# One attention and sign-weight feed-forward block: second-half projections one step later, six down-weight signs moved past attention, and pairwise probability sums on GpSimd

## The reference

```python
x = layernorm(x + attn(x))      # x is (2, 1024, 512) float32, 16 heads of 32
x = layernorm(x + ffn(x))

# attn: qkv = x @ w_qkv.T + b_qkv
#       scores = q @ k.T / sqrt(32), causal mask, softmax over the keys, @ v
#       out @ w_out.T + b_out
# ffn:  relu(x @ sign(up_weight).T * up_scale) @ sign(down_weight).T
#       * down_scale * output_scale          (512 -> 2048 -> 512)
```

## Time and profile before

| | us |
|---|---|
| three runs | 834.71, 837.71, 842.72 (median 837.71) |
| the profiled execution | 842.53, of which the span from first to last instruction is 840.8 |
| PE busy | 770.7 (92%) |
| DVE busy | 453.1 (54%) |
| ACT busy | 324.1 (39%) |
| POOL busy | 268.4 (32%) |

### The profile page before, as it was taken

How to read it: one execution, slowest core, us unless ns; L and a number is a source line. 1 busy time by engine, 2 the same in 40 slices (tenths; PEclk the granted TensorE clock), 3 DMA queues, 4 the chain that set the end, 5 groups by cost and what they waited for, 6 DMA issues and landing times.

```text
span 840.8 us, 11785 instructions
## 1 busy us (share of the span) xinstructions
PE 770.7 (92%) x4176; PEld 524.9 (62%) x4176; DVE 453.1 (54%) x1086; ACT 324.1 (39%) x631; POOL 268.4 (32%) x415
## 2 busy tenths in 40 slices
PE   6899889999999998999989958899999999999994
PEld 5688646555655465555634425478787877878883
DVE  3276455675656657657556644363339327633614
ACT  5200435454544554545545644732222223221211
POOL 5801513314223134132240241153235234423333
PEclk9999889999999999999977979999999999999997
DMA  8937452542734335425375453021001200100101
GB/s 299 295 83 216 134 139 89 141 128 61 200 101 100 116 112 143 112 79 161 89 189 164 143 196 113 1 66 63 24 13 38 88 25 13 38 2 0 51 1 50
DMA packets 44619, 85.72 MB, mean 102 GB/s; under 512 B 4880, under 2 KB 13584, under 8 KB 44432
## 3 DMA queue, kind: packets, MB, share of 16 engines
q1 hardware_dynamic: 35536, 79.72, 31.8%
q10 hardware_dynamic: 9024, 5.24, 2.2%
HBM read 55.33 MB, written 29.36 MB: 101 GB/s over the span
## 4 chain that ended last, share of the span: by engine, by line
PE 72%; DVE 14%; DMA 5%; issue 4%; ACT 2%; POOL 1%; SPq 1%; ACTq 0%; DVEq 0%; POOLq 0%
PE ps_heads L952 9%; PE ps_sum L946 8%; PE ps_unit L891 8%; PE ps_proj L853 7%; PE ps_proj L992 6%; PE ps_score L928 6%; DVE heads_sb L750 6%; PE ps_score L1007 6%; PE ps_unit L966 6%; PE ps_unit L992 5%; PE ps_heads L1007 3%; PE ps_sum L1007 3%; DVE heads_sb L752 2%; DMA qk_parts<-parts 2%; DVE ps_unit L724 2%
## 5 line engine op out<-in xcount | busy, mean ns | idle before, releaser
L636 ACT ACTIVATE probs<-ps_score 128x512 f32<-128x512 f32 (+3 forms) x360 | 171.2, 491 | 193.4 <-PE ps_score L928 185.6
L891 PE MATMUL ps_unit<-stack 96*128 96x512 f32 (+3 forms) x384 | 138.3, 369 | 14.1 <-DVE maxes L728 7.9
L724 DVE CUSTOM_DVE_ANT_0 ps_unit<-ps_unit,causal 128x128 f32<-128x128 f32 (+3 forms) x256 | 122.7, 502 | 50.4 <-PE ps_unit L891 49.2
L928 PE MATMUL ps_score<-stack 98*128 98x512 f32 (+2 forms) x360 | 136.6, 388 | 8.9 <-ACT probs L636 5.7
L559 POOL TENSOR_SCALAR_AFFINE_SELECT probs<-probs 128x128 f32<-128x128 f32 x256 | 74.7, 298 | 212.6 <-ACT probs L636 209.2
L583 POOL TENSOR_TENSOR hid_low<-hid_raw,hid_high 128x512 fp32r<-128x512 f32 x64 | 85.0, 1328 | 175.7 <-DVE hid_high L803 169.5
L728 DVE TENSOR_REDUCE maxes<-ps_unit 128x1 f32<-128x512 f32 x128 | 88.2, 689 | 85.3 <-PE ps_unit L891 84.3
L891 PEld LDWEIGHTS ps_unit<-stack 96*128 96x128 f32 x384 | 75.6, 198 | 48.7 <-DVE maxes L728 16.1
L928 PEld LDWEIGHTS ps_score<-stack 98*128 98x128 f32 x360 | 71.4, 199 | 39.6 <-ACT probs L636 20.5
L803 DVE CAST hid_high<-hid_raw 128x512 fp32r<-128x512 f32 x64 | 27.1, 425 | 121.1 <-ACT hid_raw L681 120.8
L553 POOL TENSOR_TENSOR parts<-qk_full,parts 128x512 fp32r<-128x512 f32 x32 | 41.3, 1292 | 155.8 <-ACT parts L618 155.8
(11 more groups left out here) (162 smaller groups left out, 1174.3 us busy)
## 6 DMA issues: line engine op xcount, KB each, us to landing
stack<-qk_parts SPq DMA_DIRECT2D x96, 256.0 KB, 5.0
qk_parts<-parts SPq DMA_DIRECT2D x32, 512.0 KB, 2.8
v_all<-h_even ACTq DMA_DIRECT2D x16, 256.0 KB, 3.2
v_rows<-v_all SPq DMA_DIRECT2D x8, 512.0 KB, 4.6
heads_t<-heads_sb SPq DMA_DIRECT2D x16, 256.0 KB, 2.7
raw<-up_w SPq DMA_DIRECT2D x8, 512.0 KB, 4.3
raw<-down_w SPq DMA_DIRECT2D x8, 512.0 KB, 3.8
heads_raw<-heads_t SPq DMA_DIRECT2D x4, 1024.0 KB, 5.7
```

What stands on the lines that cost most here:

```text
L636: nc.scalar.activation(probs[:, (NP * s + n) % RING, 0:width], score_bank(s, n)[:, off:off + width], ACT.Exp, scale=SCALE).then_inc(s_exp, 1)
L724: nc.vector.tensor_tensor_reduce(ps_unit[n % 3][:, 0:width], ps_unit[n % 3][:, 0:width], causal[:, HALF - width:], 1.0, NEG, ALU.add, ALU.max,
L891: nc.tensor.matmul(ps_unit[n % 3][:, 0:width], stack[s % 2][0:96, 1, f, h, i % 4 * P:(i % 4 + 1) * P], stack[s % 2][0:96, 0, c, h, 0:width ...
L928: nc.tensor.matmul(score_bank(s, n)[:, 0:width + off], stack[s % 2][0:98, 0, j // 4, h, j % 4 * P:(j % 4 + 1) * P], stack[s % 2][0:98, 1, ...
```

## The change

It has four parts. **Projections:** `BLOCK` now names for each block how many steps ahead it is made. Blocks 2 and 3 (the second half) are made one step ahead, at the start of the step, blocks 0 and 1 two steps ahead, later in the step. Before the first score only two blocks of step 1 are left, and step 6 makes two blocks of step 7. The loads of the second batch of x stand later in SP's order, and the weights of a new group are taken up in another place. **Units:** all units of the second query half with the first key half (c = 0) come before those with the second key half (c = 1), so that the first 32 units need three blocks and the last 16 the fourth; the table `MAXIMA` starts at slot 10.2 rather than 0.5, and the two shifts stand at 35.9 and 51.9 rather than 27.9 and 48.2. **Row sums:** for the four full key tiles of the second query half, POOL adds the probabilities of two key tiles (`pairs`, four tiles of 128x512 at a time), and one row-sum matmul per head takes the sum of the two. **Late part:** six of the down signs stand behind the start of the feed-forward part (with the weights stored in another order, `down_at`), `up` and `down` of chunk 0 wait for each sign apart; the first fetch of heads stands in step 6 and goes to a buffer of its own, the output projection has two banks in step 7, and its slots are 7 to 31.

```diff
-MAXIMA = ([0.5, 1.2, 2.1, 2.6, 3.1, 3.6, 10.2, 10.9, 11.6, 12.3, 13.4, 14.3, 15.2, 16.1, 17, 17.9, 18.6, 19.2,
-           24.2, 24.9, 25.6, 26.3, 27, 27.6] + [28.5 + 0.8 * u for u in range(24)])
-BLOCK = [(4.2, 0.72), (13.3, 1.25), (28.3, 0.62), (36.3, 0.66)]
-EVICT = [13.05, 28.05, 36.05, 44.05]
-KEEP = [15.8, 31, 39, 47]
-FILL = [18.5, 34, 48.2, 50]
+MAXIMA = ([10.2 + 0.55 * u for u in range(5)] + [13.4 + 0.55 * u for u in range(11)]
+          + [25.2 + 0.6 * u for u in range(5)] + [28.4 + 0.7 * u for u in range(27)])
+BLOCK = [(1, 2, 4.2, 0.72, 13.05, 15.8, 18.5), (1, 3, 13.3, 0.5, 19.65, 22.4, 24.8),
+         (2, 0, 22, 1.1, 36.05, 38.8, 41.3), (2, 1, 36.3, 0.6, 44.05, 46.8, 49.2)]
+FIRST_ADD, LAST_ADD = 4, 8
+NA = 2 * GH
-UNITS = [(h, i, c) for f in range(2) for h in range(GH) for i in range(4 * f, 4 * f + 4) for c in range(f + 1)]
+UNITS = [(h, i, c) for f in range(2) for c in range(f + 1) for h in range(GH) for i in range(4 * f, 4 * f + 4)]
-NU1 = 24
+NU1 = 33
...
             put(t + at, "pv", s, g)
-            put(t + at, "sum", s, g)
+            if g < FIRST_ADD or g >= LAST_ADD:
+                put(t + at, "sum", s, g)
+        for a in range(2):
+            for h in range(GH):
+                put(t + 25.6 + 8 * a + 0.01 * h, "add", s, GH * a + h)
+            put(t + (33, 41)[a], "sum_added", s, a)
...
-            put(t + 27.9, "shift", s + 1, 0)
+            put(t + 35.9, "shift", s + 1, 0)
             put(t + 47.2, "row_max", s + 1, 1)
-            put(t + 48.2, "shift", s + 1, 1)
+            put(t + (51.9 if s + 2 < STEPS else 48.2), "shift", s + 1, 1)
...
-    for k in range(NJOBS):
-        put(late + (4 * k - 1.5 if k > 1 else -0.2), "job", 0, k)
-        put(late + 4 * k + 6, "sign", 0, k)
+    signs = [late + 25, late + 28] + [late + 33 + 5 * k for k in range(8)] + [late + 88, late + 92]
+    signs += [FIRST_UP + 1 + 2 * k for k in range(6)]
...
-    put(last + 1, "fetch", 0)
+    put(late + 30, "fetch", 0)
+    put(last + 12, "fetch", 1)
     for i in range(4):
-        put(last + 6 + i, "split", 0, i)
+        put(last + 1.4 + i, "split", 0, i)
...
-            put(last + 12 + 4 * i + 0.33 * m, "attn", 0, 12 * i + m)
+            put(last + 7 + 6 * i + 0.5 * m, "attn", 0, 12 * i + m)
...
+                if what == "add":
+                    k = NP * s + GH * (FIRST_ADD + n // GH * 2) + n % GH
+                    pool.wait_ge(s_exp, k + GH + 1)
+                    wait(pool, s_used, NA * s + n - GH + 1)
+                    nc.gpsimd.tensor_tensor(pairs[:, n % GH, :], probs[:, k % RING, :], probs[:, (k + GH) % RING, :],
+                                            ALU.add).then_inc(s_add, 1)
...
                     wait(act, s_pv, NP * s + n - RING + 1)
+                    k = n - RING - GH * FIRST_ADD
+                    if 0 <= k < 2 * NA:
+                        act.wait_ge(s_add, NA * s + k // (2 * GH) * GH + k % GH + 1)
...
+                if what == "sum_added":
+                    for h in range(GH):
+                        rows = slice(h * HD, (h + 1) * HD)
+                        pe.wait_ge(s_add, NA * s + GH * n + h + 1)
+                        nc.tensor.matmul(ps_sum[rows, :], ones[:, :], pairs[:, h, :], start=(n == 0), stop=False,
+                                         tile_position=(0, h * HD)).then_inc(s_used, 1)
...
+                    if s == 0:
+                        pe.wait_ge(s_sign, 3 + n // 2)
```

126 lines of the change are left out of this document (74 added, 52 removed).

## The result

The changed kernel takes 810.53 us (median of 4 runs, 810.01 to 810.98) against 838.19 us before (median of 4, 834.71 to 842.72): a ratio of 0.9667, with a 95% interval of 0.962 to 0.9714. The forecast was 785 us, its range 768 to 812. The direction and the range held. The medians are 27.7 us apart, where 53 were forecast. Between the two profiled executions, of the 56.5 us of the sum 32.5 came (the span went from 840.8 to 808.3 us).

The account below looks back on a forecast made before the run. PE was taken as the bound, busy nearly throughout before the first score and in feed-forward, 93% in steps 1 to 5 at 0.96 clock. Terms -8 - 8 - 22.5 - 8 - 10 = -56.5 from 842.5 gave 786, stated 785 us; range 768 to 812.

Parts of the forecast that it names:

- Step 6, forecast -8: Step 6 gets 24 matmuls where PE had least to do; 49 us expected, -8 us (-4 to -11), nearly all clock.
- The start, -8: Before the first score: 24 matmuls go (5.5 us) and the first unit's 2.71 us stack wait shrinks; -8 us (-5.5 to -9).
- Steps 1 to 5, -4.5: Middle steps: sums, waits and clock together give -4.5 us each, so 50.2 us a step and -22.5 us for five.
- The row maxima: Steps 1 to 5: PE's wait for row maxima, 8.8 us in five steps, goes with the later shift; -1.8 us a step.
- DVE's maxima: Steps 1 to 5: of PE's 1.9 us per step waiting before units, mostly for DVE's maxima, 1.2 us goes.
- The wait of a unit at slot 25 for its stack: Steps 1 to 5: the second-half block's chain to its first unit just fits, 12.5 of 13.7 us; +0.3 us a step.
- The sums: Every step: four row-sum groups go, two come (1.8 us less), two more visits at 0.3 us; net 1.2 us less.
- Step 0, -8: Step 0: 1.2 us for sums, the 2.56 us shift-row wait, 4.3 of 6.6 us of clock; -8 us (-4 to -10).
- Step 7, -10: Step 7: 8.9 us of waits go, about 3 us for DVE comes, sums 1.2, clock 3; -10 us (-5 to -14).
- The stack comes late: Rival, chance 0.15: slow DMAs into the stack exceed the cover by 2.5 us in each of seven steps, giving 803 us.
- The clock still falls: Rival, chance 0.15: thin step starts still lose 2.2 us of clock each, steps 0 and 6 give back half; 797 us.
- POOL's additions hold the row sums: Rival, chance 0.03: additions take 3.9 us each, PE waits 7.8 us sixteen times; 911 us, slower than before.

Follow-up runs that it names:

- the fill alone: Changed kernel with step 6's fill of the stack's second-half query rows moved to slot 17.55, ahead of the first-half heads store: 808.58 us.
- the fill with the spread block: Changed kernel with step 6's fill ahead of the heads store, the last projection block spread over slots 14.6 to 24, and late-weight work moved later: 799.72 us.
- With the reader moved: Changed kernel with ACT's and POOL's splitting of the second batch's x at slots -130 to -123, not -136 to -122, loads unmoved: 807.37 us.
- the run with the shift early and the fill ahead: Changed kernel with the second-half shift at slot 48.2, not 51.9, and block 1's stack fill at 48.1, ahead of the shift's DMAs: 817.27 us.
- both parts taken back: Changed kernel without POOL's additions (all row sums matmuls on the probabilities) and with the second-half shift at slot 48.2: 832.7 us.
- the fill behind the shift: Changed kernel with the second-half shift at slot 48.2 in every step, so the stack fill at 49.2 stands behind the shift's DMAs: 827.47 us.

## Why the prediction was right, and where it was not

The kernel got faster for the reasons given in steps 0 to 5 and 7. That the number lies in the range is in part luck: it is 1.5 us from the upper end, and the rivals that set this end (803 and 797 us) are not what happened. The start and step 6 missed their own bounds on the slow side. The near bounds of all stages together would have been 842.5 - 25.5 = 817 us, and the range stopped at 812.

**Step 6, forecast -8, measured +7.3.** This is where the sum failed. The step that failed is "I count it from below: a new middle step, 50.2, less 24 matmuls ... plus 2.5 us of waits for the division and the stack: 49", with "nearly all of it is the clock". I counted the order of a paired step. In step 6 SP has a store that waits for DVE ahead of the fill, which I had not read off SP's order, and the wait was 5.15 us. And I gave the whole clock back to a stretch of which I only knew that it has fewer projections: 17.1 us of half clock stand in it, 8.6 us lost. Both are shown: the fill alone takes 3.8 us off the step, the fill with the spread block 10.3. From the 54.0 us that are left to my 49, 0.9 is the middle step itself and 3.0 are waits (5.5 of idle PE against 2.5); the last us or so is open. The same paragraph expects the two blocks to land "just where PE had least to do"; the stretch beside the division stayed empty of them.

**The start, -8 against -1.9.** Outside its bounds. The 24 matmuls and the first unit's wait (2.71 to 0.7) went as priced. What failed is that I priced the loads of x being issued later at a gain only. I had named them as what the first unit no longer stands behind; I did not follow them to their reader, ACT, and to what is queued behind it there, the V stores. With the reader moved the first score stands at 84.5, -6.9.

**Steps 1 to 5, -4.5 against -3.6 per step.** The signs held: no wait for the row maxima, no half clock at all (some 2.0 back, 1.7 taken). By the earlier trace rows and the windows after, PE's idle time fell by 1.0 a step (18.0 to 12.9 us in five), where the terms for it, -1.8 - 1.2 + 1.1 + 0.3, gave 1.6; its busy time fell by 2.6, where sums and clock, 1.2 + 1.7, gave 2.9. So the mis-sized part is mostly the idle time:

- The row maxima. I read 8.8 us off the weight load's row as PE's wait; PE's own was 7.2, 1.4 a step. All of it went, but not all by the late shift: the run with the shift early and the fill ahead pays 0.74 of wait and 0.6 to 0.7 a step. The rest had gone with the moved projections and units: with both parts taken back the wait is 3.7 us in five steps, with the additions alone in the kernel before 7.1. Which of the moved pieces did it, the six early units most likely, no run shows.
- DVE's maxima were not the gain of 1.2: the wait before units fell from 9.5 to 6.6 us in five steps (0.6 a step), and 0.6 a step stands anew at the transpose of the first half (2.8 us).
- The wait of scores for exponentials grew from 1.1 to 3.5 us, 0.5 a step; for it and the moved units I had 1.1.
- The wait of a unit at slot 25 for its stack, +0.3, did not come. The one that comes is at the first unit, slot 10, for another block: 0.8 us together in two of the five steps, and with the fill behind the shift 1.87 us and the clock.

The sums gave 1.4 for 1.2. The Trainium skill's TensorEngine Tiling (Array Packing), Key Properties, says that a change of the tiling mode drains TensorE. The trace agrees with the 0.2 us of a visit. The dearer of my two readings of it, 0.5 a visit, would have made the sums worth 0.8 a step; that is not what the run without them shows.

**Step 0, -8 against -10.9.** Just beyond its bounds (-4 to -10): its half clock went entirely, 0.89 to 1.00, where I had taken two thirds (4.3 of 6.6), and the wait of 2.56 us for the shift rows is gone; a new one of 1.5 us for V stands there.

**Step 7, -10 against -9.0.** Within its bounds, with its pieces off in both directions. The heads' load was worth 8.1 (I had 8.9 for it and the output projection's bank together), the wait for DVE was 6.4 and not 3: I had set eight operations against seven slots of ACT's pace, but PE reached that point 5.2 us after the step's start, and the last two splits stood behind the whole division.

**Feed-forward, 0.** ACT's busy time rose from 66.9 to 72.2 us and the span stayed.

**Rivals.** *The stack comes late* came in step 6 alone, and from a queue, not from a slow DMA (median 4.6 us to landing, 4.9 in the earlier trace rows). *The clock still falls* came in steps 6 and 7, not at the starts of steps 1 to 5. *POOL's additions hold the row sums* did not. Doubled, they make the kernel slower than before, and sooner than its price had it: the break-even was put at 2.8 us per addition, and 2.57 gave 860.9 us. The reason is another as well, since the row sums wait for only 6.4 us of it. Of the stated signs, the first score near 83, the clock above 0.9 in step 6 and no wait of PE over 4 us in step 7 proved wrong, and each pointed at its cause.

## What to carry to other kernels

When a step is copied from a regular stage to an edge stage, read the order of every queue again at the edge: a store or load that waits there stood in front of everything behind it here, on SP and on ACT alike. A stretch in which PE has only work paced by another engine can cost twice, its idle time and the clock behind it, and work that was already there, spread into it, gave both back here. A part that is taken back for a test can change the order of another queue as well: read the waits of the test's own profile before its time is put down to the part.
